# Row maxima three slots before the boundary, setup steps reordered, and a second row group for the last scores

## The reference

```python
def ffn(x):                                   # butterfly = 10 linear stages
    h = einsum('bsd,dh->bsh', x, W_exp) + b_exp
    h = butterfly(h, up_weights, 1024)
    h = gelu(h + up_bias, approximate=False)
    h = butterfly(h, down_weights, 1024)
    return einsum('bsh,hd->bsd', h, W_con) + b_con + down_bias
def attn(x):
    Q, K, V = (einsum('bsd,hkd->bhsk', x, w) for w in (WQ, WK, WV))
    scores = where(causal, einsum('bhqd,bhkd->bhqk', Q, K) / 4, -inf)
    return einsum('bhsv,hdv->bsd', softmax(scores) @ V, WO)
x = x + 0.5 * ffn(layernorm(x)); x = x + attn(layernorm(x)); x = x + 0.5 * ffn(layernorm(x))
```

## Time and profile before

| | before |
|---|---|
| median of 3 runs | 2031.27 us |
| the profiled execution | 2032.39 us |
| span in its trace | 2030.7 us |
| PE busy | 1960.6 us (97%) |
| DVE busy | 1692.8 us (83%) |
| ACT busy | 1362.3 us (67%) |
| POOL busy | 342.3 us (17%) |
| mean granted clock | 0.992 |

### The profile page before, as it was taken

The page is one execution under the profiler, slowest core; times in us unless marked ns, Lnnn a source line. Parts: engine busy times, 40 slices in busy tenths (PEclk is TensorE's granted clock), DMA queues, the critical chain, the costliest instruction groups (busy, mean ns, idle before and its releaser), DMA issues.

```text
span 2030.7 us, 59085 instructions
## 1 busy us (share of the span) xinstructions
PE 1960.6 (97%) x24312; PEld 1206.0 (59%) x24312; DVE 1692.8 (83%) x3661; ACT 1362.3 (67%) x1640; POOL 342.3 (17%) x787
## 2 busy tenths in 40 slices
PE   2799999999999999999999999999999999999999
PEld 1677777655555555555555555555555555569998
DVE  7755566599999999999999999999999999736663
ACT  3422122288888888888888888888888888774444
POOL 6400000010111111011111101011110111124444
PEclk9899999999999999999999999999999999999999
DMA  7112111221111111111111111111112111101110
GB/s 192 42 67 82 50 50 50 85 67 40 42 51 42 47 46 43 42 40 52 41 46 44 45 44 40 52 41 45 41 45 47 40 51 33 51 28 61 53 53 22
DMA packets 93245, 104.26 MB, mean 51 GB/s; under 512 B 25552, under 2 KB 55856, under 8 KB 92720
## 3 DMA queue, kind: packets, MB, share of 16 engines
q1 hardware_dynamic: 92272, 100.23, 17.4%
q0 software_dynamic: 704, 0.25, 0.2%
HBM read 70.54 MB, written 29.36 MB: 49 GB/s over the span
## 4 chain that ended last, share of the span: by engine, by line
PE 91%; DVE 3%; SPq 2%; ACT 1%; DMA 1%; issue 1%; POOL 0%; POOLq 0%; ACTq 0%; DVEq 0%
PE PS L1167 32%; PE PS L1288 32%; PE PS L1144 7%; PE PS L1268 6%; PE PS L1114 6%; PE PS L1347 4%; PE PS L1219 2%; PE PS L1080 1%; PE PS L1138 1%; SPq L388 1%; DVE OA L829 1%; POOL QT L600 0%; ACT OA L631 0%; SPq L392 0%; DVE OA L934 0%
## 5 line engine op out<-in xcount | busy, mean ns | idle before, releaser
L722 ACT ACTIVATE PG<-PS 128x1024 f32<-128x1024 f32 (+1 forms) x1152 | 1117.1, 977 | 239.0 <-PE PS L1268 176.8
L958 DVE TENSOR_REDUCE MXP<-PS 128x1 f32<-128x512 f32 x1792 | 1099.2, 684 | 18.2 <-PE PS L1167 18.1
L1268 PE MATMUL PS<-QT,KT 50*128 50x512 f32 (+1 forms) x2304 | 811.1, 432 | 0.0
L1167 PE MATMUL PS<-KT,QT 48*128 48x512 f32 (+3 forms) x2304 | 797.1, 431 | 2.8 <-DVE MXP L958 2.3
L1288 PE MATMUL PS<-PG,VH 128*17 128x128 f32 x16896 | 726.1, 276 | 0.1
L1288 PEld LDWEIGHTS PS<-PG,VH 128*17 128x17 f32 x16896 | 400.2, 97 | 415.5 <-issue 367.2
L1167 PEld LDWEIGHTS PS<-KT,QT 48*128 48x128 f32 x2304 | 340.8, 184 | 251.2 <-issue 142.4
L1268 PEld LDWEIGHTS PS<-QT,KT 50*128 50x128 f32 x2304 | 339.5, 185 | 10.3 <-issue 10.1
L954 DVE CUSTOM_DVE_ANT_0 PS<-PS,MASK 128x128 f32<-128x128 f32 (+3 forms) x512 | 249.1, 505 | 73.4 <-PE PS L1167 67.7
L580 POOL TENSOR_SCALAR_AFFINE_SELECT PG<-PG 128x128 f32<-128x128 f32 x512 | 136.4, 292 | 999.3 <-ACT PG L722 998.5
L652 ACT ACTIVATE PG<-PS,GB 128x512 f32<-128x512 f32 x128 | 89.8, 706 | 161.9 <-PE PS L1114 161.9
(11 more groups left out here) (122 smaller groups left out, 1263.6 us busy)
## 6 DMA issues: line engine op xcount, KB each, us to landing
QT<-q_parts SPq DMA_DIRECT2D x256, 64.0 KB
KT<-k_parts SPq DMA_DIRECT2D x256, 64.0 KB
q_parts<-OA SPq DMA_DIRECT2D x16, 512.0 KB, 2.8
QT<-q_parts SPq DMA_DIRECT2D x256, 32.0 KB
k_parts<-OA SPq DMA_DIRECT2D x16, 512.0 KB, 4.9
KT<-k_parts SPq DMA_DIRECT2D x256, 32.0 KB
o_parts<-OS SPq DMA_DIRECT2D x128, 64.0 KB
OA<-o_parts SPq DMA_DIRECT2D x32, 256.0 KB
```

Source lines behind the costliest of these rows:

```text
L722: nc.scalar.activation(PB[n % 2][half][:, :, q0:TILE], PS[:, half * 1024:half * 1024 + 1024].rearrange("p (k q) -> p k q", k=2)[:, :, q0:T ...
L958: nc.vector.tensor_reduce(dst, bank(b), AX.X, ALU.max).then_inc(mx_red, 1)
L1167: mm(bank(4 + qs % 2 if b is None else b, w), q[0:SC, (BT * place(j) + qs) * P:(BT * place(j) + qs + 1) * P].bitcast(f32r), k[0:SC, c * TI ...
L1268: last = mm(PS[:, (2 * half + k) * 512 + q0:(2 * half + k + 1) * 512], CK[0:SM, kb * P:(kb + 1) * P].bitcast(f32r), CQ[0:SM, place(j) * TI ...
```

## The change

AHEAD becomes LAST_OF_FIRST + 3 = 21. MX0 of tile 6 (eight maxima, slots 21 and 22) is then empty: four leave step t = 7, four leave step t = NT; the same eight are computed in the head loop, whose slots 553 and 554 now have maxima. `split_slot` moves two slots later for both groups.

Setup: ACT issues up stage 1 and half of stage 2 ahead of its first wait; POOL makes `ident` before it issues stage 3; the unused copy `identb` goes. Up mixing stage 0 runs in block pairs as they are folded, partly inside `finish_stats`. GB and OB move behind `low_weights`, OB behind the whole down mixing. ACT loads the gelu table by a one-column activation before it is needed, runs down mixing stage 0 ahead of `gb_rdy`, and alternates single gelus with parts of stages 1 and 2. POOL sets NK[32:64] to one ahead of CK.

End of the head loop: from slot 555 on, the second score matmul of each half reads NK and NQ instead of CK and CQ. For that SP also writes the last head's two maximum parts to NQ, in four more DMAs behind each of the last two `load_m`, with semaphores `m_ld_n`.

```diff
-AHEAD = 23
+FIRST_ROWS = 4
+LAST_OF_FIRST = LAST[ORDER[FIRST_ROWS - 1]] + 1
+AHEAD = LAST_OF_FIRST + 3
...
-            if t == NT - 1:
-                soon = soon[:LAST_LEFT]
             if t == NT:
-                late = [(NT - 2, i) for i in range(LAST_LEFT, len(MX0[NT - 2]))]
+                late = []
...
-            for s in range(INNER):
-                if s != UP_BY_POOL:
-                    inner_weights(sp, up_w, FU["w"], s, in_up[s])
+            for s in (0, 2, 4, 5, 6):
+                inner_weights(sp, up_w, FU["w"], s, in_up[s], range(4) if s == 2 else None)
...
-                for q in range(BT):
-                    sp.dma_start(CQ[SC:SM, c0:c0 + S // 2].rearrange("a (b q t) -> a b q t", b=half, q=BT)[:, :, q, :],
-                                 MT[g][q * Q32:(q + 1) * Q32, :]).then_inc(m_ld[g], 16)
+                for to, sig in ((CQ, m_ld[g]), (NQ, m_ld_n[g])) if i >= 2 * (H - 1) else ((CQ, m_ld[g]),):
+                    rows = to[SC:SM, c0:c0 + S // 2].rearrange("a (b q t) -> a b q t", b=half, q=BT)
+                    for q in range(BT):
+                        sp.dma_start(rows[:, :, q, :], MT[g][q * Q32:(q + 1) * Q32, :]).then_inc(sig, 16)
...
-            inner_weights(nc.gpsimd, up_w, FU["w"], UP_BY_POOL, in_up[UP_BY_POOL])
             link(nc.gpsimd.memset(ident[:, :], 0.0))
...
+            inner_weights(nc.gpsimd, up_w, FU["w"], UP_BY_POOL, in_up[UP_BY_POOL])
...
+            nc.gpsimd.memset(NK[NEXT // 2:NEXT, :], 1.0)
             nc.gpsimd.memset(CK[NEXT // 2:NEXT, :], 1.0).then_inc(att_init, 1)
...
+            inner_weights(nc.scalar, up_w, FU["w"], 1, in_up[1])
+            inner_weights(nc.scalar, up_w, FU["w"], 2, in_up[2], range(4, 8))
             act.wait_ge(const_rdy, 1)
...
-            take_fold(range(0, HB - 2))
-            std(0, slice(0, 2 * BT))
-            take_fold(range(HB - 2, HB))
-            act.wait_ge(in_d, 48)
-            act.wait_ge(fold_ev, HB)
-            mix_a_side(0, range(3))
+            for b in range(HB):
+                take_fold((b,))
+                if b == 1:
+                    act.wait_ge(in_d, 48)
+                if b % 2:
+                    act.wait_ge(fold_ev, b + 1)
+                    mix_a_side(0, (0,), (b - 1, b))
+                if b == 3:
+                    std(0, slice(0, 2 * BT))
+            mix_a_side(0, (1, 2))
...
+            nc.scalar.activation(SQRT_FIRST[:, :], ident[:, 0:1], ACT.Gelu)
+            act.wait_ge(in_wc, 16)
+            mix_a_side(1, (0,))
             act.wait_ge(gb_rdy, 1)
...
-                    for k in range(3):
-                        gelus(0, 0, (2 * k, 2 * k + 1))
-                        mix_a_side(1, (k,))
+                    gelus(0, 0, (0, 1))
+                    for b, k, mixed in ((2, 1, range(0, 2)), (3, 1, range(2, 4)), (4, 1, range(4, 8)),
+                                        (5, 2, range(0, 4))):
+                        mix_a_side(1, (k,), mixed)
+                        gelus(0, 0, (b,))
+                    mix_a_side(1, (2,), range(4, 8))
...
-            nc.vector.tensor_copy(identb[:, :], ident[:, :])
...
-            finish_stats(0, slice(0, 2 * BT), 2 * BT, 2 * BT)
+            dve.wait_ge(in_d, 48)
+            finish_stats(0, slice(0, 2 * BT), 2 * BT, 2 * BT, lambda: mix_v_side(0, (0,), range(0, 4)))
             normalize(XN, 0, None)
-            dve.wait_ge(in_d, 48)
-            dve.wait_ge(fold_ev, HB)
-            mix_v_side(0, range(3))
+            mix_v_side(0, (0,), range(4, 8))
+            mix_v_side(0, (1, 2))
             take_transposed_parts(0, seq_f(0))
-            dve.wait_ge(mix_v, 3 * HB)
-            nc.vector.tensor_tensor(GB[:, :], T1[:, :, D], UB[:, :], ALU.add).then_inc(gb_rdy, 1)
...
+                last_slots = h * NCH + n >= H * NCH - AHEAD
+                if half == 0 and h * NCH + n == H * NCH - AHEAD:
+                    pe.wait_ge(m_ld_n[0], 16 * BT)
+                if half == 0 and last_slots and c == j and j == ORDER[FIRST_ROWS]:
+                    pe.wait_ge(m_ld_n[1], 16 * BT)
...
-                    last = mm(PS[:, (2 * half + k) * 512 + q0:(2 * half + k + 1) * 512], CK[0:SM, kb * P:(kb + 1) * P].bitcast(f32r),
-                              CQ[0:SM, place(j) * TILE + q0:(place(j) + 1) * TILE].bitcast(f32r), start=True, stop=True)
+                    kt, qt = (NK, NQ) if last_slots and k else (CK, CQ)
+                    last = mm(PS[:, (2 * half + k) * 512 + q0:(2 * half + k + 1) * 512], kt[0:SM, kb * P:(kb + 1) * P].bitcast(f32r),
+                              qt[0:SM, place(j) * TILE + q0:(place(j) + 1) * TILE].bitcast(f32r), start=True, stop=True)
```

More of the change, by code:

```diff
@@ L390, in inner_weights @@
             else:
-                for r in range(2 * n):
+                for r in part or range(2 * n):
                     eng.dma_start(d[r:P:2 * n], w).then_inc(sig, 16)
@@ L623, in std, with mix_a_side @@
                 nc.scalar.activation(LN[:, 3, cols], LN[:, 2, cols], ACT.Sqrt).then_inc(std_rdy, 1)
-            def mix_a_side(down, stages):
+            def mix_a_side(down, stages, blocks=range(HB)):
                 for k, b, ia, ib, wa, wb in mix_steps(down):
-                    if k not in stages:
+                    if k not in stages or b not in blocks:
                         continue
@@ L832, in normalize, with mix_v_side @@
                 last.then_inc(xn_rdy, 1)
-            def mix_v_side(down, stages):
+            def mix_v_side(down, stages, blocks=range(HB)):
                 for i, (k, b, ia, ib, wa, wb) in enumerate(mix_steps(down)):
-                    if k not in stages:
+                    if k not in stages or b not in blocks:
                         continue
+                    if k == 0 and not down:
+                        dve.wait_ge(fold_ev, (b | 1) + 1)
                     if k:
@@ L978, in _ @@
                     projected_parts(t - 1)
-                for item in pair(late, "h5") if t < NT else late[0] + late[1]:
+                for item in pair(late, "h5") if t < NT else ():
                     maximum0(*item)
```

25 lines of the change are left out of this document (12 added, 13 removed).

## The result

The changed kernel takes 2025.41 us (median of 15 runs) against 2031.44 for the kernel before: ratio 0.9965, 95% interval 0.9951 to 0.9979. By this ratio that is 7.1 us or 0.35% less (the two medians lie 6.0 apart), so within 0.5%, where 17.7 us less were forecast, and the median is 0.4 us above the range of 2004 to 2025. The runs of the changed kernel go from 2019.9 to 2034.4, but for one disturbed run of 3330 us, those of before from 2029.7 to 2039.9, and the profiled execution (2030.13 us, span 2028.4) lies 4.7 us above its own median.

A forecast was written before the change was run, and what follows sets the result against it. PE was taken to bound the head loop, a chain of loads and DVE the setup. Setup - 12.8, then - 2.9, - 1.8, + 4.5 and - 4.7 sum to - 17.7 us: 2013.6 us from a median of 2031.27, range 2004 to 2025.

The forecast's parts named there:

- Parts 1 to 3: Setup up to the first up block: product, up mixing and what stood ahead of `low_weights`, 5.0, 2.1 and 5.3 us less.
- part 1: Setup up to the product: loads moved to ACT and an earlier DVE start give 5.0 us less, bounds 0 and 5.3.
- part 2 and 3: Setup: up mixing stage 0 half hidden behind folding, 2.1 us less; `in_bias` wait, OB and GB off the path, 5.3 less.
- The second rival: Setup gives less: PE waits for POOL's down product (6.6 instead of 12.8 us), or transfers bind later stages; chance 0.22.
- Part 4: Step t = 0: gelu table load hidden, ACT's down stage 0 ahead and finer interleaving, 2.6 us less, bounds 1.28 and 5.4.
- Part 5: POOL's second memset delays the first tile's bias addition, so the third y block waits: 2.2 us more.
- Part 6: First phase, eight maxima less: 0.8 us in t = 7, 2.1 in t = NT; they cost 0 in slots 553 and 554.
- Part 7: Head loop: diagonals of scores and maxima meet in slots 0, 15 and 21 instead of slot 28 alone, 1.8 us less.
- Part 8: Later split: its load lands 0.15 us late at each of 30 group starts, 4.5 us more, bounds 0 and 15.
- The first rival: Late split loads make group-start waits decide: at 1.2 us each the kernel takes 2045 us; chance 0.05.
- Part 9: Last 21 slots: paired scores in two row groups leave ACT the bound at 2.19 us a slot; 4.7 us less, stall included.
- The third rival: End of head loop: scores in different row groups run one behind the other, no gain, 2020.2 us; chance of 0.08.

The follow-up runs named there:

- dd_late: `best22` with the load of DD (outer down stages) moved behind the inner ones in SP's queue, with its own semaphore: 2009.5 us, ratio 0.9897.
- ahead22: The changed kernel with the maxima 22 instead of 21 slots ahead: 2010.2 us, ratio 0.9895 to the kernel before.
- setup_only: The changed kernel with 23 slots ahead as before and no second row group, leaving only the reordered setup: 2026.3 us, ratio 0.9966.
- ahead20: The changed kernel with the maxima 20 instead of 21 slots ahead: 2321.0 us in one run.
- ahead23: The changed kernel with 23 slots ahead as before, keeping the reordered setup and the second row group: 2016.1 us, ratio 0.9917.
- tail_off: The changed kernel without the second row group for the last 21 slots and without copies to NQ: 2027.2 us, ratio 0.9971.
- bias_first: The changed kernel with POOL adding the first tile's output bias ahead of its two memsets instead of behind: 2025.8 us, ratio 0.9964.
- best22: The changed kernel with 22 slots ahead and POOL adding the first tile's bias ahead of its two memsets: 2012.3 us, ratio 0.9901.
- dve_last: The changed kernel with the down product's last stage on DVE, behind its down mixing, instead of on POOL: 2030.8 us, ratio 0.9985.
- ahead_only: The kernel before with the maxima 21 instead of 23 slots ahead and nothing else changed: 2040.8 us, ratio 1.0035.
- pool_last_out: The changed kernel with POOL's last down product stage replaced by a memset, leaving out part of the computation: 2014.4 us, ratio 0.9911.

## Why the prediction was wrong, point by point

**Parts 1 to 3** (- 12.4) hold by and large. The product ends at 23.4 instead of 28.2, 4.9 us earlier (part 1: 5.0). MUL starts 11.5 us earlier and PE follows; part 2 and 3 together gave 6.7 of 7.4, with 1.8 us of waiting for x on the way. In the other kernels with this setup, `dd_late` (46.7) apart, the first up block even starts at 42.7 to 43.8. There DVE's up mixing runs ahead of POOL's fourth stage, as in `ahead22`; in this trace it is the other way round, and the mixing takes 10.6 us instead of 8.0. The second rival had later stages bound by transfers, with 0 to 2 us from part 1. That did not happen: the 4.9 us are nearly the 5.3 of issuing time that moved to ACT.

**Part 4** (- 2.6) is the step of the setup that failed: the slowing of DVE's down mixing beside POOL got no price. Between the first up block and the first y block nothing was gained: 2.7 us were lost (in `ahead22` 5.0: what POOL is refused in the up mixing it takes in the down mixing, and the first y block starts at 74.1 all the same). The table load is hidden, as forecast. But "POOL is multiplying beside it" was taken as a reason for a smaller gain, not priced. Both engines work longer beside each other, since DVE came 11.5 us forward and the end of POOL's product only 5.4 (66.90 to 61.54). Before, one mixing instruction was held, for 2.6 us beside the last instruction of the earlier trace rows on POOL; now three are held for 2.6 to 3.2 us each. What is held is waited for by ACT, and by PE through the gelus. Besides, PE was granted 1.2 GHz from 62.2 to 72.5 us, from the last up block through most of `fold_down`, where before it was so only from 78.9 to 82.3. The Trainium skill, page "SBUF — State Buffer", section "Who interferes with whom", says that a VectorE instruction with two SBUF inputs and a GpSimd one that reads SBUF contend for a shared pair of ports, and that the second to start blocks until the first is through. The traces agree on the hold: 3.19 us where 0.47 is the rule, and no such hold beside POOL's memset. But POOL's 7.51 us for 64 columns spans a run of DVE instructions and not one. The second rival named "a DVE that is busier", at - 6.6 for the setup; `setup_only` measured - 6.9. Its time was right, in part by luck, since a share of the 6.9 is what the first phase gives or takes for an open reason. Its mechanism, PE waiting for POOL's product, did not come in the changed kernel's trace, nor in that of `dd_late`: there the product ends at 61.5 or 61.6 and PE stands until 63.4 or 63.5 for the gelu behind the held mixing. But it came in the seven other traces with this product (`ahead20`, `ahead22`, `ahead23`, `setup_only`, `tail_off`, `bias_first`, `best22`), where the product ends at 64.1 to 64.9 and PE waits 6.1 to 6.9 us for it, with the mixing over at 66.8 to 67.5. In `setup_only`:

```profile
64.72 1.97 PE L1112 MATMUL PS<-ident,V 128*128 128x128 f32 x8 [6.91 <-POOLq L549]
```

Product and mixing hold each other there, and `dve_last`, with no mixing held and a product as late, is no earlier at the first y block.

**Part 5** (+ 2.2) holds: a stall of 2.17 us where it was put.

**Part 6** (- 2.9): the wait ahead of the projections was worth 2.5 us (transposes to projections 5.1 us in the trace before, from 386.03 to the 391.15 of the earlier trace rows, and 2.6 after). In the trace with 22 slots the clock, too, stays up in the projections, 2.3 us more. In the trace of the changed kernel 1.2 GHz was granted from 396.7 to 403.6 us in place of 389.5 to 396.3; there head 0 pays for it (90.6 us against 87.6). Whether it does differs by trace and not by the number of slots, as said under `ahead22`. Where no load is late, one slot less is worth having: `ahead22` is 4.5 us faster than `ahead23` by the ratios, about the 4.7 that parts 6 and 7 forecast for two slots less, though the clock has a part in it (projections of 6.16 us against 8.6 in the traces).

**Part 7** (- 1.8) holds: slots 0, 15 and 21 are 0.08, 0.06 and 0.06 us shorter, slot 28 is 0.06 longer, 1.9 us over heads 1 to 14. Slot 16 is 0.09 longer with 21 slots alone, 1.3 us in all; why is open.

**Part 8** (+ 4.5) is the step that decided. The point was right within 0.1 us: slack and shift do cancel. What failed is that a landing was taken as one number, and its issue as never late. Together they scatter by 1.5 us; around a slack of nothing, the late ones are paid and the early ones aren't, and 28 waits came to 8.3 us, 0.30 each. And a wait had only its own length as a price. Of the waits seen at group starts with 21 slots, those of up to 1.2 us were followed by nothing; the two longest, 1.38 us in `ahead_only` and 1.65 in `bias_first` (1.06 and 1.14 us of idle time in the rows), by 1.2 GHz. The windows around the second:

```profile
core 0: us, PE busy (x) PEld busy (x) DVE busy (x) ACT busy (x) POOL busy (x), PEclk, DMA share, GB/s
785.40:792.20 6.80, 5.66 (x76) 3.13 (x75) 5.79 (x12) 3.99 (x4) 0.19 (x1) 1.00 0.21 58
792.20:799.00 6.80, 6.80 (x64) 3.25 (x64) 4.01 (x7) 3.24 (x5) 1.08 (x4) 0.50 0.02 7
```

That head took 93.1 us instead of 88.0. It is also a reason for the wide scatter of the runs with 21 slots, though no run isolated that. The first rival ("the waits decide", 0.05) gave 1.2 us a wait a price of 36 us, the waits alone. No run had waits of that mean; at 2.8 us a wait in `ahead20` the 30 waits alone are 84 us, and it lost 290. Its mechanism is what took most of the gain, at a quarter of the wait that it asked for, so its chance was set too low.

**Part 9** (- 4.7) was wrong in both terms. Of its readings, the start of a maximum and a score within 0.01 us stands in the trace, though not in the earlier trace rows, and the three slots to row 1 take 7.1 us in the kernel before, not 7.3. The load arrived when forecast: row 1 started 8.34 us behind slot 555 (8.4). But the stall of 2.27 us was followed by 1.2 GHz from 1768.9 to 1775.7 us (for 3.4 us in `bias_first` and `dve_last`, and not at all in `pool_last_out`, with the same stall), and slots 558 and 559 take 5.2 and 3.6 us instead of 2.9 and 3.0 in `ahead22`: slots 555 to 561 lost 2.6 us, where the stall was put at 1.1 more and the gains in these slots at 2.2. The full slots gained more: ACT was to bound them at the 2.19 us of the earlier trace rows, but that row is two exponentials of 1.03 us with a pause of 0.13 between them, too short to be shown in it. Fed in time, 14 take

```profile
1770.33 13.42 ACT L737 ACTIVATE PG<-PS 128x1024 f32<-128x1024 f32 x14 [1.24 <-PE PS L1290]
```

so 0.96 us each with one short one of a diagonal slot among them (in `ahead23`). The second of a slot starts 0.93 us behind the first, with no pause, and the first of the next slot 1.05 behind that. A slot takes 1.98, in which PE is busy throughout, not the estimated 1.8 of PE nor the 2.19 of ACT: 0.46 us less a slot, not 0.26. What the Trainium skill says in "PSUM Bottleneck" (page "TensorEngine Tiling (Array Packing)") names the right neighbour: ACT has next to no pause left (some 0.1 us of 1.98, an estimate from 0.93 and 1.05), but PE is the bound here. The third rival falls: two scores in different row groups do run beside each other.

**Sum.** The step that failed is part 8: a fixed landing and no price beyond the wait, + 4.5 us, where one slot more of slack gave back 14.3. Setup - 6.9 instead of - 12.8; second row group - 10 with its load in time, instead of - 5.8 without a stall; the maxima alone + 7.1 instead of - 0.2. The first two errors nearly cancel: `ahead22`, which has all three parts of the change with one slot more of slack, measured - 21.4, where the prediction without its waits had - 23.3. That these come so near is luck in part. What the changed kernel lacks against `ahead22`, 14.3 us, lies mainly in the waits and in the clock behind them.

Of the signs named for "right", short idle time at slots 0 and 18, the stall at slot 558 and the projections behind the rounding of x came. The first up block came 11.5 us earlier, short of 12 (14 to 15 in most other traces), and the fold matmuls at 68.7 instead of about 62. Of those named for "wrong", the longer stretches at 1.2 GHz came, and `fold_down` waiting for POOL in seven other traces. The fastest kernels of the study are `ahead22` and `dd_late`, both 1.0% faster than before, with no difference between them that the runs can tell.

## What to carry to other kernels

Before a producer is moved towards its consumer, give the DMA between them its late landing as a price, not its mean: at a slack of zero every late one is paid, and one slot of slack (2.4 us) was worth 14 us here. On a TensorE-bound loop an idle stretch costs more than its length once the granted clock falls behind it: the head behind one wait of 1.38 us took 6.7 us more in `ahead_only`, so a few of them can outweigh a real gain elsewhere. And when work on VectorE comes forward, look at what it now stands beside on GpSimd: an instruction there with two inputs in SBUF and one of GpSimd that reads SBUF took turns, each for its whole length.

## What the runs showed of the hardware that was not expected

- Small loads of one kind in a quiet loop (DMA share 0.17 before, 0.18 after) landed 1.75 to 3.1 us behind their issue in the kernel before and to 3.2 in `ahead20`, by what their semaphore records.
- Behind 28 of the 30 waits of 2.25 to 3.8 us in `ahead20` PE was granted 1.2 GHz, for up to 37.5 us, although it was busy all that time (30.70 of 30.70 us in the window shown). Where the clock fell in the head loop of the other kernels it came back after 3.4 to 13.7 us.
- A POOL instruction on 64 columns lasted 7.51 us beside DVE's mixing; alone a like one took 0.68.
- One load of 24 KB kept SP for 8.1 us, and with it moved SP stood as long at the next load (7.6 us).
